# Key-block differences and the scaling of a head pair's outputs, moved between two engines of a four-layer transformer kernel

## The chip, the cores and the metric

The kernel runs on one NeuronCore of a Trainium2 chip. Its engines work side by side and meet at semaphores: TensorE (PE, with its weight loads shown apart as PEld), VectorE (DVE), ScalarE (ACT), GpSimd (POOL), and the DMA queue of SyncE (SP). The metric is the device time of one execution in microseconds (us); lower is better.

## The reference, cut to what matters

Four layers of attention and feed-forward over one sequence of 2048 positions and width 128, each with a layer norm ahead and a residual behind. Three of the attention blocks are softmax attention with 16 heads of 64: one plain, one causal, one with a region mask and a bias by feature. In short:

```python
Q = jnp.einsum('btd,hkd->bthk', x, W_Q) + b_Q
K = jnp.einsum('btd,hkd->bthk', x, W_K) + b_K
V = jnp.einsum('btd,hkd->bthk', x, W_V) + b_V
scores = jnp.einsum('bqhk,bshk->bhqs', Q, K) / jnp.sqrt(jnp.asarray(d_head, x.dtype))
# second block: dot = jnp.where(causal, dot, -inf); last block: region mask and a bias
attn = jax.nn.softmax(scores, axis=-1)
out_h = jnp.einsum('bhqs,bshk->bqhk', attn, V)
return jnp.einsum('bqhk,hdk->bqd', out_h, W_O) + b_O
```

The feed-forward blocks are a mixture of eight experts, a gated channel mix, a ternary and a binarised two-layer network. The change doesn't touch them, nor the short algebraic attention of the third layer.

## The kernel before, in words

The three softmax blocks are one program, built three times from a table of when each piece of work is due (`LAYERS`, here called attention 0, 1 (causal) and 2). Each walks through 8 pairs of heads; the two heads of a pair share the 128 partitions (64 each). The 2048 queries are cut into four chunks of 512 (c = 0 to 3), the keys into tiles of 128. A pair takes 16 cycles in attention 0 and 2, and 10 in attention 1; a cycle (number g within the pair) handles four key tiles:

- PE multiplies the scores of a tile as a sum of products (`Kh·Qh`, `Kh·Ql`, `Kl·Qh`, and a product of auxiliary rows that carries the row maxima and masks), ACT takes the exponentials into a ring of eight tiles (`work`, L1000), DVE adds them up into the sum of a chunk (`acc`, L1230 and L1242), PE multiplies them with `V`.
- The row maxima come ahead of the scores, in units: PE multiplies queries with the difference of each two neighbouring key tiles (`Kd`, matmul `ps<-Kd,Qh`), ACT keeps the positive part (L1008, into `over` or, for a cycle's second unit, into `wexp`), PE then multiplies the queries with the first tile of each two (the "base", matmul `ps<-Kh,Qh`), and DVE adds both and takes the maximum (`tops`, L1264: two instructions per segment, results in `mpart` and at a row's end in `mcol`). In the causal block POOL cuts the blocks on the diagonal (L1110 in a unit, L1123 in the exponentials).
- While a pair is worked on, the projections of the next pair are made one by one. For a chunk of K or Q: PE multiplies, ACT writes the high part (`Kh`, `Qh`, L972), DVE the rest (`Kl`, `Ql`, L1177), and for K the difference of neighbouring tiles (`Kd`, L1181).
- When a chunk of queries is through, PE sums `acc` over the partitions, ACT copies the sums, SP packs them (`dcomp`), DVE inverts them (L1206), SP spreads the inverses over all partitions (`rden`), and one cycle later the chunk's outputs `oT` are scaled into `oN` (L1212, function `normalise`). PE multiplies `oN` with the output weights, DVE adds the product to `x` (L1201).

Every engine has its own program, written in the same order of cycles. Within a cycle DVE does: the maxima of the unit in slot 0 (left from the cycle before), the last sum of the cycle before, the maxima of slot 1, a `normalise` if one is due (cycles `mul_at`: 6, 10, 14 and 2 of the next pair in attention 0 and 2; 4, 7, 0 and 2 of the next pair in attention 1), a reciprocal if due, then the sums and projection jobs mixed. The chunks of K of the next pair are due in cycles 0, 1, 2, 3 (attention 0 and 2) and 1, 3, 4, 8 (attention 1). An engine runs its instructions in order, so whatever stands ahead of the maxima on DVE delays them, and PE waits for the maxima (`top_ready`) before it may overwrite their banks. The first pair of each attention has its projections and first maxima in an `opening` with nothing else beside them.

## Time and profile before

| | |
|---|---|
| three runs | 3916.33, 3919.72, 3926.92 us (median 3919.72) |
| the profiled execution | 3920.88 us, of which its span is 3919.2 us |
| PE busy | 3633.6 us (93%) |
| DVE busy | 2901.8 us (74%) |
| ACT busy | 2270.1 us (58%) |
| POOL busy | 196.1 us (5%), 273 instructions |
| granted TensorE clock, mean | 0.972 |

The three attention blocks take 84 to 1365 us, 1508 to 2346 us and 2557 to 3858 us of the span. The layers' other work lies between. A row of a timeline is: start in us from the span's start, duration in us, engine, line, operation, output and inputs by the program's names, how many instructions, and in brackets how long the engine stood idle before it and who ended that. Two neighbouring instructions of one engine overlap a little: the next one starts before the last one's end is recorded.

### The profile page before, as it was taken

To read this page: it belongs to the slowest core of one execution; us is meant where nothing else is said; L and a number is where in the kernel's file an instruction comes from. 1 tells how busy PE (TensorE), PEld (TensorE's weight loads), DVE (VectorE), ACT (ScalarE), POOL (GpSimd) and SP (SyncE) were. 2 spreads that over 40 slices of the span, in tenths; PEclk is the share of its full clock that TensorE was granted. 3 is DMA by queue.
4 is the path that set the end of the run, shared out by engine and by line. 5 is a ranking of instruction groups with operands and counts; after the bars stand their busy time and mean duration, and the time that the engine had idled before them with its cause. 6 is when DMAs were issued, how large, how long until landed. Compare 5 with 4: busy or idle time off the path is not lost.

```text
span 3919.2 us, 65392 instructions
## 1 busy us (share of the span) xinstructions
PE 3633.6 (93%) x24661; PEld 1907.6 (49%) x24661; DVE 2901.8 (74%) x5821; ACT 2270.1 (58%) x2635; POOL 196.1 (5%) x273
## 2 busy tenths in 40 slices
PE   4999999999999958999999996699999999999997
PEld 2455455454554424555555554245545455554544
DVE  5777878778787777777777765477777877778784
ACT  3666666666666516655655652466666666666663
POOL 1000000000000001212222210000000000000000
PEclk9999999999999989999999997899999999999998
DMA  1000000000000000000000000000000000000000
GB/s 51 7 9 10 9 11 8 9 10 9 9 7 7 9 13 7 15 15 12 15 12 13 10 15 3 19 7 12 7 9 10 10 9 10 9 10 8 7 10 17
DMA packets 44398, 44.27 MB, mean 11 GB/s; under 512 B 16466, under 2 KB 30554, under 8 KB 43834
## 3 DMA queue, kind: packets, MB, share of 16 engines
q1 hardware_dynamic: 44090, 40.09, 3.3%
q8 instruction: 202, 3.31, 0.3%
q14 instruction: 106, 0.87, 0.1%
HBM read 37.56 MB, written 1.70 MB: 10 GB/s over the span
## 4 chain that ended last, share of the span: by engine, by line
PE 79%; DVE 11%; issue 4%; ACT 3%; DMA 1%; SPq 1%; POOL 0%; DVEq 0%; ACTq 0%
PE ps L565 76%; DVE over L1264 2%; DVE acc L1242 2%; DVE wexp L1264 1%; DVE x L1402 1%; ACT Kh L972 1%; ACT work L1000 1%; PE ps L863 1%; PE ps L874 1%; DVE stats L1150 1%; DVE Kd L1181 1%; PE ps L554 1%; SPq L475 0%; PE ps L903 0%; DMA auxQ<-mrow 0%
## 5 line engine op out<-in xcount | busy, mean ns | idle before, releaser
L1000 ACT ACTIVATE work<-ps 128x1024 f32<-128x1024 f32 (+1 forms) x1344 | 1276.8, 994 | 950.6 <-PE ps L565 943.9
L1242 DVE TENSOR_TENSOR acc<-acc,work 128x1024 f32<-128x1024 f32 (+2 forms) x1152 | 1353.5, 1175 | 49.4 <-ACT work L1000 11.8
L565 PE MATMUL ps<-work,V 128*64 128x512 f32 (+3 forms) x5376 | 1239.9, 581 | 0.0
L565 PEld LDWEIGHTS ps<-work,V 128*64 128x64 f32 x5376 | 452.8, 138 | 547.2 <-issue 452.7
L565 PE MATMUL ps<-Qh,Kh 64*128 64x512 f32 (+3 forms) x2688 | 654.2, 482 | 32.4 <-issue 10.8
L1264 DVE CUSTOM_DVE_ANT_0 over<-ps,over,mpart 128x512 f32<-128x512 f32 (+3 forms) x642 | 422.3, 695 | 310.4 <-PE ps L565 310.2
L565 PE MATMUL ps<-Qh,Kl 64*128 64x512 f32 (+3 forms) x2688 | 525.7, 385 | 0.0
L565 PE MATMUL ps<-Ql,Kh 64*128 64x512 f32 (+3 forms) x2688 | 522.5, 383 | 0.0
L565 PE MATMUL ps<-auxQ,auxK 64*128 64x512 bf16 (+3 forms) x2688 | 518.6, 380 | 0.0
L1264 DVE CUSTOM_DVE_ANT_0 wexp<-ps,wexp 128x512 f32<-128x512 f32 (+1 forms) x632 | 376.5, 635 | 24.1 <-PE ps L565 19.2
L565 PE MATMUL ps<-Kh,Qh 64*128 64x512 f32 (+2 forms) x1520 | 343.1, 464 | 35.8 <-DVE mpart L1264 14.5
L1008 ACT ACTIVATE over<-ps 128x1024 f32<-128x1024 f32 (+1 forms) x321 | 314.2, 979 | 26.3 <-PE ps L565 26.3
L1008 ACT ACTIVATE wexp<-ps 128x1024 f32<-128x1024 f32 x318 | 328.3, 1032 | 0.0
L565 PE MATMUL ps<-Kd,Qh 64*128 64x512 f32 (+2 forms) x1504 | 289.2, 454 | 38.9 <-DVE mpart L1264 29.5
L565 PEld LDWEIGHTS ps<-Qh,Kh 64*128 64x128 f32 x2688 | 260.1, 188 | 125.1 <-ACT work L1000 60.3
L565 PEld LDWEIGHTS ps<-Kh,Qh 64*128 64x128 f32 x1520 | 139.4, 186 | 337.3 <-issue 236.2
L565 PEld LDWEIGHTS ps<-auxQ,auxK 64*128 64x128 bf16 x2688 | 133.0, 93 | 345.3 <-issue 342.2
L565 PEld LDWEIGHTS ps<-Qh,Kl 64*128 64x128 f32 x2688 | 255.6, 185 | 51.5
L565 PEld LDWEIGHTS ps<-Ql,Kh 64*128 64x128 f32 x2688 | 258.2, 187 | 19.9
L565 PE MATMUL ps<-yT,wqk 128*64 128x512 f32 x768 | 214.0, 616 | 13.3 <-DMA wqk<-in_wqk 12.3
L565 PEld LDWEIGHTS ps<-Kd,Qh 64*128 64x128 f32 x1504 | 142.3, 188 | 131.9 <-DVE mpart L1264 62.2
L1177 DVE SCALAR_TENSOR_TENSOR Ql<-ps,bqk,Qh 128x512 fp32r<-128x512 f32 x96 | 72.0, 750 | 167.8 <-ACT Qh L972 167.8
(188 smaller groups left out, 2599.3 us busy)
## 6 DMA issues: line engine op xcount, KB each, us to landing
rden<-inverse_sums SPq DMA_DIRECT2D x192, 128.0 KB, 2.8
auxQ<-mrow SPq DMA_DIRECT2D x384, 1.0 KB
wqk<-in_wqk SPq DMA_DIRECT2D x24, 128.0 KB, 2.5
dcomp<-rden SPq DMA_DIRECT2D x192, 2.0 KB
wv<-in_wv SPq DMA_DIRECT2D x24, 64.0 KB, 2.3
inverse_sums<-rcomp SPq DMA_DIRECT2D x96, 4.0 KB, 1.3
work<-in_mlp_w SPq DMA_DIRECT2D x1, 1024.0 KB
work<-in_c_aux SPq DMA_DIRECT2D x1, 1024.0 KB, 4.9
```

The costliest lines, as they stand in the source:

```text
L554: mm = pe.transpose(ps[:, t // TPC, (t % TPC) * P:(t % TPC + 1) * P], work[:, t // TPC, (t % TPC) * P:(t % TPC + 1) * P], ident[:])
L565: return pe.matmul(o, w, m, start=start, stop=stop, skip_group_check=True)
L863: pe.matmul(bank(m % 4), wm[:, 2 * n, j * P:(j + 1) * P], yv[:, c * CH:(c + 1) * CH], start=True, stop=True).then_inc(s["h_psum"], 1)
L874: mm = pe.matmul(ps[:, 4 + c, t * P:(t + 1) * P], work[:, j * 4 + c, t * P:(t + 1) * P], wm[:, 2 * n + 1, j * P:(j + 1) * P], start=(j == ...
L972: act.activation(dst[p][:, c * CH:(c + 1) * CH], bank(b), ACT.Identity, bias=bqk[:, p, w:w + 1]).then_inc(s["hi_ready"], 1)
L1000: act.activation(work[:, 2 * e:2 * e + 2, q0:CH], ps[:, b:b + 2, q0:CH], ACT.Exp, scale=L.scale).then_inc(s["p_ready"], 1)
L1008: act.activation(excess_of(sl)[:, :, 0:w], ps[:, b:b + 2, 0:w], ACT.Relu)\
L1150: ins = dve.bn_stats(stats[:, t, :], x[:, t, :])
L1177: dve.scalar_tensor_tensor(lo[:, cols], bank(b), bqk[:, p, w:w + 1], hi[:, cols].bitcast(F32), ALU.add, ALU.subtract).then_inc(s["lo_ready ...
L1181: dve.tensor_tensor(Kd[p][:, c * (CH // 2):(c + 1) * (CH // 2)].rearrange("p (n k) -> p n k", k=P), tiles[:, 2 * c:2 * c + 2, 1 - L.base, ...
L1242: dve.tensor_tensor(o, o, work[:, slots[two]:slots[two] + 2, q0:CH], ALU.add).then_inc(s["acc_ready"], 1)
L1264: dve.tensor_tensor_reduce(clipped[:, h2, col:col + w], ps[:, b0 + h2, col:col + w], clipped[:, h2, col:col + w], 1.0, start, ALU.add, ALU ...
```

## The change

POOL now runs a program for all three attention blocks instead of the causal one alone. It computes the differences `Kd` and the scaling `oN`, both with its `tensor_tensor`; the same two instructions are gone from DVE. The waits stay with the moved instructions: `Kd` on the high part of K (`hi_ready`), `oN` on the spread inverses (`rden_in`), on the output's copy (`o_ready`) and on the product with the last `oN` (`op_ready`). In POOL's cycle the scaling stands first, then the diagonal cuts, then the cuts of the units, then the differences. (The blank and re-indented lines of the diff change nothing else.)

```diff
--- before.py
+++ after.py
@@ -1092,27 +1092,43 @@
                 pool.memset(selq[h2 * DH:h2 * DH + 1, 0:NREG], 1.0).then_inc(cleared, 1)
             pool.wait_ge(cleared, 3)
 
-            def cuts(L):
+            def attention(L):
+
 
 
                 s = A[L.n]
                 K = L.K
-                zero, low = pool.to_reg(0.0), pool.to_reg(-BIG)
                 none = selq[:, P - 1:P].rearrange("p (m o) -> p m o", m=1).to_broadcast([P, 2, P])
+
+                def differences(h, c):
+                    p = h % 2
+                    pool.wait_ge(s["hi_ready"], 8 * h + L.qk_index("K", c) + 1)
+                    tiles = Kh[p][:].bitcast(F32).rearrange("p (n two k) -> p n two k", two=2, k=P)
+                    pool.tensor_tensor(Kd[p][:, c * (CH // 2):(c + 1) * (CH // 2)].rearrange("p (n k) -> p n k", k=P),
+                                       tiles[:, 2 * c:2 * c + 2, 1 - L.base, :], tiles[:, 2 * c:2 * c + 2, L.base, :],
+                                       ALU.subtract).then_inc(s["kd_ready"], 1)
+
+                def normalise(h, c):
+                    pool.wait_ge(s["rden_in"], 32 * (NC * h + c + 1))
+                    pool.wait_ge(s["o_ready"], NC * h + c + 1)
+                    at_least(pool, s["op_ready"], NC * h + c)
+                    pool.tensor_tensor(oN[:], oT[:, c % 2, :], rden[:], ALU.mult).then_inc(s["on_ready"], 1)
 
                 def cut_unit(h, u, slot):
                     if L.cuts_to[u + 1] > L.cuts_to[u]:
                         pool.wait_ge(s["relu_ready"], L.NR * h + L.relus_to[u] + 1)
-                    for _, t, col, b, nb, _, ends in L.units[u]:
-                        if ends:
-                            o = excess_of(slot)[:, :, col + (nb - 1) * P:col + nb * P]
-                            last_alone = t % 2 == 0
-                            pool.affine_select(o, none if last_alone else o, [[0, 2], [-1, P]], ALU.is_ge,
-                                               low if last_alone else zero, base=0, channel_multiplier=1)\
-                                .then_inc(s["unit_cut"], 1)
+                        for _, t, col, b, nb, _, ends in L.units[u]:
+                            if ends:
+                                o = excess_of(slot)[:, :, col + (nb - 1) * P:col + nb * P]
+                                last_alone = t % 2 == 0
+                                pool.affine_select(o, none if last_alone else o, [[0, 2], [-1, P]], ALU.is_ge,
+                                                   low if last_alone else zero, base=0, channel_multiplier=1)\
+                                    .then_inc(s["unit_cut"], 1)
 
                 def cycle(x):
-                    if L.main(x):
+                    for m, c in L.due(L.mul_at, x):
+                        normalise(m, c)
+                    if L.main(x) and L.causal:
                         for j in range(4):
                             tile = 4 * x + j
                             _, q0, diag = L.steps[2 * (x % L.G) + j // 2][1][j % 2]
@@ -1124,14 +1140,21 @@
                                     .then_inc(s["diag_cut"], 1)
                     for sl, m, u in L.units_in(x):
                         cut_unit(m, u, sl)
-
-                for what, u, _, b in L.opening_items():
+                    for sl, kind, m, c in L.jobs_in(x):
+                        if kind == "K":
+                            differences(m, c)
+
+                for what, u, c, b in L.opening_items():
                     if what == "unit":
                         cut_unit(0, u, int(b != MAXB))
+                    elif u == "K":
+                        differences(0, c)
                 for at in range(L.X):
                     cycle(at)
 
-            cuts(LAYERS[1])
+            zero, low = pool.to_reg(0.0), pool.to_reg(-BIG)
+            for L in LAYERS:
+                attention(L)
 
 
         @block.vector
@@ -1176,11 +1199,6 @@
                         hi, lo, w = (Qh[p], Ql[p], 0) if kind == "Q" else (Kh[p], Kl[p], 1)
                         dve.scalar_tensor_tensor(lo[:, cols], bank(b), bqk[:, p, w:w + 1], hi[:, cols].bitcast(F32),
                                                  ALU.add, ALU.subtract).then_inc(s["lo_ready"], 1)
-                        if kind == "K":
-                            tiles = Kh[p][:].bitcast(F32).rearrange("p (n two k) -> p n two k", two=2, k=P)
-                            dve.tensor_tensor(Kd[p][:, c * (CH // 2):(c + 1) * (CH // 2)].rearrange("p (n k) -> p n k", k=P),
-                                              tiles[:, 2 * c:2 * c + 2, 1 - L.base, :], tiles[:, 2 * c:2 * c + 2, L.base, :],
-                                              ALU.subtract).then_inc(s["kd_ready"], 1)
                     elif kind == "mt":
                         top = ps[0:2 * TPC, b, 0:P]
                         dve.wait_ge(s["mt_psum"], NC * h + c + 1)
@@ -1204,12 +1222,6 @@
                 def inverse(h, c):
                     dve.wait_ge(s["comp_in"], 32 * (NC * h + c + 1))
                     dve.reciprocal(rcomp[:], dcomp[:]).then_inc(s["inv_ready"], 1)
-
-                def normalise(h, c):
-                    dve.wait_ge(s["rden_in"], 32 * (NC * h + c + 1))
-                    dve.wait_ge(s["o_ready"], NC * h + c + 1)
-                    at_least(dve, s["op_ready"], NC * h + c)
-                    dve.tensor_tensor(oN[:], oT[:, c % 2, :], rden[:], ALU.mult).then_inc(s["on_ready"], 1)
 
                 def sums_of(x):
 
@@ -1284,8 +1296,6 @@
                     for sl, m, u in before_:
                         if sl == 1:
                             tops(m, u, slot=1)
-                    for m, c in L.due(L.mul_at, x):
-                        normalise(m, c)
                     for m, c in L.due(L.inv_at, x):
                         inverse(m, c)
                     for which in sums[:1]:
```

The programs of PE, ACT and SP are the same row for row. DVE's has 201 rows fewer, POOL's has 116 more.

On DVE, in cycles 2 and 3 of a pair in attention 0 (`Kl` belongs to the next pair, `over` and `mcol` to the row maxima). Before:

```order
L1242 TENSOR_TENSOR acc<-acc,work 128x1024
L1177 SCALAR_TENSOR_TENSOR Kl<-ps,bqk,Kh 128x512
L1181 TENSOR_TENSOR Kd<-Kh 128x256
L1242 TENSOR_TENSOR acc<-acc,work 128x1024
L1264 ISA over,mcol<-ps,over,mpart 128x512
L1264 ISA mcol 128x1
```

And now:

```order
L1200 SCALAR_TENSOR_TENSOR Kl<-ps,bqk,Kh 128x512
L1254 TENSOR_TENSOR acc<-acc,work 128x1024
L1276 ISA over,mcol<-ps,over,mpart 128x512
L1276 ISA mcol 128x1
L1276 ISA over,mcol<-ps,over,mpart 128x512
```

The sum and the maxima follow the low part of K at once; line numbers have shifted.

On POOL, in cycles 0 to 2 of a pair in attention 1 (`work` are the diagonal cuts of the exponentials, `over` those of a unit). Before:

```order
L1123 AFFINE_SELECT work<-work 128x2x128 [waits p_ready_1] x4
L1110 AFFINE_SELECT over<-over 128x2x128 [waits relu_ready_1]
L1110 AFFINE_SELECT over<-selq 128x2x128 [waits relu_ready_1]
L1123 AFFINE_SELECT work<-work 128x2x128 [waits p_ready_1] x4
L1110 AFFINE_SELECT over<-over 128x2x128 [waits relu_ready_1]
```

And now:

```order
L1139 AFFINE_SELECT work<-work 128x2x128 [waits p_ready_1] x4
L1124 AFFINE_SELECT over<-over 128x2x128 [waits relu_ready_1]
L1124 AFFINE_SELECT over<-selq 128x2x128 [waits relu_ready_1]
L1107 TENSOR_TENSOR Kd<-Kh 128x256 [waits hi_ready_1]
L1115 TENSOR_TENSOR oN<-oT,rden 128x512 [waits op_ready_1,o_ready_1,rden_in_1]
L1139 AFFINE_SELECT work<-work 128x2x128 [waits p_ready_1] x4
L1124 AFFINE_SELECT over<-over 128x2x128 [waits relu_ready_1]
```

The difference of cycle 1 and the scaling of cycle 2 now stand between two units' cuts and the four diagonal cuts of cycle 2.

## Rows read from the trace of the kernel before

**Rows 1.** The page: the chain that ended last, share of the span by engine.
```profile
PE 79%; DVE 11%; issue 4%; ACT 3%; DMA 1%; SPq 1%; POOL 0%; DVEq 0%; ACTq 0%
```

**Rows 2.** Windows of attention 0, 1, 2: length; PE, PEld, DVE, ACT, POOL busy; clock; DMA.
```profile
84.00:1365.00 1281.00, 1264.70 (x8446) 639.15 (x8444) 1004.68 (x1729) 810.12 (x903) 0.00 (x0) 1.00 0.03 9
1508.00:2346.00 838.00, 784.22 (x6032) 450.02 (x6030) 609.65 (x1450) 495.84 (x616) 178.79 (x243) 0.98 0.04 13
2557.00:3858.00 1301.00, 1278.45 (x8746) 652.03 (x8744) 1009.09 (x1738) 811.92 (x903) 0.00 (x0) 1.00 0.03 9
```

**Rows 3.** Waits in attention 0 (us, times, longest); the last row reads alike in attention 2.
```profile
DVE Kl L1177 <- ACT Kh L972: 50.6, 28, 3.2
...
PE ps L565 <- DVE mcol L1264: 5.3, 15, 0.4
```

**Rows 4.** Waits in attention 1.
```profile
PE ps L565 <- DVE mpart L1264: 35.9, 50, 1.3
```

**Rows 5.** Timeline, attention 0, end of cycle 2 and start of cycle 3.
```profile
598.62 0.75 DVE L1177 SCALAR_TENSOR_TENSOR Kl<-ps,bqk,Kh 128x512 fp32r<-128x512 f32 x1 [1.47 <-ACT Kh L972]
599.29 0.41 DVE L1181 TENSOR_TENSOR Kd<-Kh 128x256 fp32r<-128x256 f32 x1
...
599.51 0.50 PE L565 MATMUL ps<-Kh,Qh 64*128 64x512 f32 x2
...
599.62 1.22 DVE L1242 TENSOR_TENSOR acc<-acc,work 128x1024 f32<-128x1024 f32 x1
...
600.76 0.75 DVE L1264 CUSTOM_DVE_ANT_0 over<-ps,over,mpart 128x512 f32<-128x512 f32 x1
...
602.24 0.50 PE L565 MATMUL ps<-Kh,Qh 64*128 64x512 f32 x2 [0.38 <-DVE mcol L1264]
```

**Rows 6.** Timeline, attention 1, end of cycle 1 and start of cycle 2.
```profile
1846.10 0.75 DVE L1177 SCALAR_TENSOR_TENSOR Kl<-ps,bqk,Kh 128x512 fp32r<-128x512 f32 x1 [1.41 <-ACT Kh L972]
1846.76 0.41 DVE L1181 TENSOR_TENSOR Kd<-Kh 128x256 fp32r<-128x256 f32 x1
...
1847.87 0.41 POOL L1123 TENSOR_SCALAR_AFFINE_SELECT work<-work 128x256 f32<-128x256 f32 x1 [3.94 <-ACT work L1000]
...
1848.59 1.22 DVE L1242 TENSOR_TENSOR acc<-acc,work 128x1024 f32<-128x1024 f32 x1
1848.73 0.50 PE L565 MATMUL ps<-Kh,Qh 64*128 64x512 f32 x2 [0.76 <-DVE mpart L1264]
...
1851.21 0.46 PE L565 MATMUL ps<-Kd,Qh 64*128 64x256 f32 x2 [1.14 <-DVE mpart L1264]
```

**Rows 7.** Timeline, attention 1: two cuts on POOL, asked of POOL alone.
```profile
1768.52 0.41 POOL L1110 TENSOR_SCALAR_AFFINE_SELECT wexp<-selq 128x256 f32<-128x256 bf16 x1 [1.66 <-ACT wexp L1008]
1768.88 1.39 POOL L1110 TENSOR_SCALAR_AFFINE_SELECT wexp<-wexp 128x256 f32<-128x256 f32 x1
```

**Rows 8.** Timeline, the same stretch, asked of DVE alone.
```profile
1768.57 1.43 DVE L1242 TENSOR_TENSOR acc<-acc,work 128x1024 f32<-128x1024 f32 x1
```

**Rows 9.** Timeline, attention 0, DVE and the DMA queue: cycles 1 and 2.
```profile
747.88 1.14 SPq L489 DMA_DIRECT2D rden<-inverse_sums  x2
...
749.87 2.55 DVE L1242 TENSOR_TENSOR acc<-acc,work 128x1024 f32<-128x1024 f32 x2
...
756.03 0.69 DVE L1212 TENSOR_TENSOR oN<-oT,rden 128x512 f32<-128x512 f32 x1
```

**Rows 10.** DMA issues: KB each, median us from issue to landing.
```profile
rden<-inverse_sums SPq DMA_DIRECT2D x192, 128.0 KB, 2.8
```

**Rows 11.** Timeline, opening of attention 0: the first product with the differences.
```profile
56.74 0.69 ACT L972 ACTIVATE Qh<-ps,bqk 128x512 fp32r<-128x512 f32 x1 [0.17 <-PE ps L565]
...
58.30 0.50 PE L565 MATMUL ps<-Kd,Qh 64*128 64x512 f32 x2 [1.60 <-DVE Kd L1181]
```

**Rows 12.** The chain in order of time, end of attention 0.
```profile
1376.99 0.70 DVE oN L1212
...
1377.83 1.99 PE ps L565 x16
```

## The prediction

> **What bounds the kernel now.** I read the windows of the three attention blocks first. They hold 3420 of 3919 us, and in attention 0 and 2 PE is busy 1264.70 of 1281 and 1278.45 of 1301 us, with DVE at 78% [rows 2]. There only 16 and 23 us are left to be won on PE. Attention 1 is the looser one: PE is busy 784.22 of 838 us, 54 us are left, and DVE has only 73%. So DVE is nowhere full; what counts is where PE waits for one result of it. The chain that ended last agrees: 79% PE, 11% DVE [rows 1]. Next the waits. In attention 0 PE stands 5.3 us in 15 waits behind the maxima `mcol`, the same in attention 2, and in attention 1 it stands 35.9 us in 50 waits behind the maxima `mpart` [rows 3, 4]. Last the timelines of those waits, to see what stands ahead of the maxima on DVE.
>
> In attention 0 it is this: DVE waits 1.47 us for `Kh`, makes `Kl`, then `Kd`, then one sum, and only then both maxima of `over`. PE waits 0.38 us for them at 602.24, though its base product (599.51, 0.50 long) was ready at 600.01 and the first maximum began at 600.76 [rows 5]. This happens behind the cycles 2 and 3, in which the last two chunks of K are due: 2 times for each of the 7 next pairs, 14 times, which fits the 15 waits. In attention 1 `Kd` stands directly ahead of the maxima, and PE waits 0.76 us and then 1.14 us [rows 6]; three of the four chunks of K there are due at a cycle's end, so 3 x 7 = 21 times.
>
> **The differences on DVE go.** There are 3 x 8 x 4 = 96. Each is recorded with 0.41 us, but its step in DVE's stream, start to start, is 599.62 - 599.29 = 0.33 us [rows 5], and 1847.10 after 1846.76 reads the same. Only that step can be given back.
> - Attention 0: 14 x 0.33 = 4.6 us, since the wait of 0.38 us is longer than the step. After the move the maxima would start at 600.43, still behind PE's 600.01, so the whole step arrives. A smaller wait behind cycle 1 gives perhaps 0.1 x 7 = 0.7 us. Sum 5.3 us.
> - Attention 2, whose row of waits reads the same: 5.3 us.
> - Attention 1: 21 x 0.33 = 6.9 us.
> - The other 96 - 12 - 49 = 35 differences lie where DVE waits for ACT or PE next; nothing comes back there.
>
> **The openings.** In attention 0 PE waits 1.60 us for the fourth `Kd` until 58.30 [rows 11]. DVE makes `Kl` and `Kd` in turn; GpSimd makes only `Kd`, from each `Kh` on. The first product also needs `Qh`, which ends at 56.74 + 0.69 = 57.43; with 0.15 us for the hand-over PE starts at about 57.6, 0.7 us earlier. Twice that for attention 2, and for attention 1, with one difference ahead of PE instead of four, I give 0.3 us (estimate). Sum 1.7 us.
>
> **The scalings on DVE go.** They are also 96, of 0.69 or 0.70 us [rows 9, 12]. They stand behind the maxima of their cycle, ahead of sums, and DVE comes to the next maxima with idle time; PE waits for `mpart` and `mcol`, not for sums. I cost their removal at nothing, and hold up to 2 us of gain as the good end.
>
> **What GpSimd takes for them.** The trace has no two-input instruction on GpSimd. The nearest is the diagonal cut, one input, 256 columns: 0.41 us alone [rows 7]. How much of it is reading can be seen beside it: a DVE sum that started 0.05 us after the cut took 1.43 us [rows 8] instead of 1.22 [rows 5]. So the cut held up a sum by 0.21 us and 256 columns of one input are read in about 0.21 us (0.8 ns per column), with 0.20 us fixed. From below, `Kd` costs no less than the cut, 0.41 us, and `oN` no less than on DVE, 0.69 us. From above, twice and four times the cut: 0.82 and 1.64 us. I take fixed part plus reads: `Kd` 0.20 + 2 x 0.21 = 0.62 us, `oN` 0.20 + 4 x 0.21 = 1.04 us. The first is nearest to its row. The Trainium skill (GPSIMD Engine Reference, Elementwise — side-by-side cycle accounting) has 4497 ns for 2048 columns, which as an estimate would make about 0.56 and 1.12 us of the columns alone; no run here shows it yet, and the sum below would be worse by under 1 us with it.
>
> **Whom that disturbs.** The next cut on GpSimd, 1768.88, took 1.39 us instead of 0.41 [rows 7]: it stood behind the DVE sum, which also reads two operands from SBUF. So the two block each other, in both directions, and the question is what DVE runs while GpSimd reads.
> - `Kd` on GpSimd can start when `Kh` is there, and this is when `Kl` starts on DVE: DVE waited for `Kh` in all 28 cases of attention 0 (50.6 us) [rows 3]. `Kl` reads one operand from PSUM. Its step is 0.67 us (598.62 to 599.29), so with 0.62 us `Kd` is over when the sum begins. Upper end, 0.82 us: the sum waits some 0.15 us, 28 times in attention 0 and 2, 4.2 us lost.
> - `oN` can start when `rden` lands: second issue at about 748.5, 2.8 us more, 751.3 [rows 9, 10]. DVE runs two sums from 749.87 to 752.42, in the new order from 749.54 to 752.1. GpSimd waits for the second one and runs beside the maxima (PSUM and one SBUF operand). DVE ran this scaling at 756.03, so there are 4 us of slack for the product that needs it.
> - In attention 1 GpSimd now has `Kd` and then `oN` ahead of the four cuts of cycle 2. `Kh` is there at 1846.1, so they end at 1846.1 + 0.62 + 1.04 = 1847.8; the first cut began at 1847.87 [rows 6]. Just in time. A cut that begins a little later would still be reading when the sum of 1848.59 (in the new order 1848.26) starts, and what follows that sum are maxima that PE waits for: I charge the 0.21 us of a cut's reading for most of the 7 pairs, 1.2 us.
> - At the end of each attention nothing hides the scaling: `oN` 0.70 us, then PE [rows 12]. 3 x (1.04 - 0.70) = 1.0 us lost; upper end 2.8 us.
>
> The rule that speaks against this change is in the Trainium skill (SBUF — State Buffer, Who interferes with whom): a DVE instruction with two SBUF inputs and a GpSimd instruction that reads SBUF exclude each other, the one that comes second being blocked until the first one has finished. The trace agrees for GpSimd as the second; as the first, it held the sum up by 0.21 us of its 0.41, so only while it reads. By the full length `Kd` would still be over with `Kl`, and the sum stays.
>
> **Sum.** 5.3 + 5.3 + 6.9 + 1.7 - 1.2 - 1.0 = 17.0 us gained. With the low ends of GpSimd's times it is 19 us (21 with 2 us for the scalings), with the high ends 5.3 + 5.3 + 6.9 + 1.7 - 4.2 - 1.2 - 2.8 = 11.0 us. The profiled execution took 3920.88 us, 1.2 above the median of 3919.72; the sum against it gives 3903.9, and against the median, which I predict from, 3902.7: 3903 us.
>
> **Rivals.**
> - No change that can be told (3908 to 3931; a measurement of this kernel tells 0.3%, 12 us). Something takes back what is won: GpSimd's times are at their upper ends, or `oN` slips in between two sums. With 1.04 us held, the sum behind it starts 1 us late; in cycle 1 to 2 of [rows 9] DVE has no idle time before the maxima at all, so PE would lose up to 1 us, 14 times in attention 0 and 2. 17 - 14 leaves 3 us: 3917. For it: `rden` lands within a microsecond of a gap between sums. Against: the landing lies inside the second sum, not ahead of it.
> - Slower: GpSimd's difference is far slower than its cut, say 1.4 us (for instance because it writes the rounded 32-bit format, which no GpSimd row here does). Then it still reads when `Kl` is through, and the sum starts at 598.62 + 1.4 = 600.0 instead of 599.62: the maxima are 0.4 us later than before, 28 times, 11 us, plus the lost gain; in attention 1 `Kd` and `oN` together last over 3.5 us and the cuts of cycle 2 come 2 us late, of which PE would see about 1 us 7 times; the three ends cost 5 us (2.5 us for `oN` instead of 0.7), the openings 1.5 us each; the 6.9 us of attention 1 stay won. 3919.7 + 11 + 7 + 5 + 3 - 7 = 3939. It decides from about 1.0 us of `Kd` on: 0.67 us of `Kl` plus the 0.33 us that the step gives back. Against it: the cut's 0.41 us.
> - More than I count: in attention 1, PE's waits total 35.9 us, and maxima that come earlier might also free sums and exponentials behind them. 25 us, 3895.
>
> **How the numbers follow.** Forecast (gain 11 to 20 us, 3899 to 3909) 0.52; more 0.06; no change 0.30; slower 0.12. Faster by over 0.3% means under 3908: nearly all of the forecast and the third rival, 0.57. Within 0.3%: 0.31. Slower: 0.12. The range leaves out the slower case and part of the larger gain: 3894 to 3924.
>
> **What would show it.** No `Kd` or `oN` on DVE; DVE busy down by 96 x (0.41 + 0.69) = 106 us, POOL up by 96 x (0.62 + 1.04) = 160 us. In attention 0, DVE's sum starts right behind `Kl`, about 0.67 us after it, and PE's 5.3 us for `mcol` nearly vanish. In attention 1 PE's wait for `mpart` falls by 6 us. The window of attention 0 shortens by 6 us, of attention 1 by 6, of attention 2 by 5. Wrong it would be if DVE's sums grow above 1.22 us on the average, if `Kd` on GpSimd takes over 1 us, or if PE's waits name POOL.

## The result, and the profile after

The changed kernel takes 3900.66 us (median of 10 runs, 3897.33 to 3907.19) against 3919.17 us before (10 runs, 3911.76 to 3926.92). The medians are 18.5 us apart, 0.47%. The measured ratio is 0.9945, with a 95% interval of 0.9928 to 0.9963. The forecast was 3903 us. The two profiled executions have spans of 3919.2 and 3899.2 us, 20.0 us apart, and all comparisons of stretches below add up to that.

The page first: busy time and the chain that ended last, to be read against [rows 1].

```profile
PE 3622.7 (93%) x24661; PEld 1905.0 (49%) x24661; DVE 2820.0 (72%) x5629; ACT 2270.6 (58%) x2635; POOL 393.5 (10%) x465
...
PE 81%; DVE 10%; issue 4%; ACT 3%; DMA 1%; SPq 1%; POOL 0%; POOLq 0%; DVEq 0%; ACTq 0%
```

DVE is busy 82 us less (forecast 106) and POOL 197 us more (forecast 160); PE has 2 points more of the chain and DVE one less. PE does the same 24661 matmuls in 3622.7 us of busy time instead of 3633.6. So 10.9 of the 20.0 us are matmuls that ran faster, and 9.1 us are PE standing less. The windows of the three attentions after (columns as in [rows 2]):

```profile
84.00:1362.00 1278.00, 1266.14 (x8454) 638.87 (x8452) 982.15 (x1671) 809.87 (x903) 67.13 (x59) 1.00 0.03 9
1502.00:2333.00 831.00, 778.80 (x6112) 448.07 (x6112) 589.14 (x1411) 502.72 (x623) 231.23 (x306) 1.00 0.05 13
2544.00:3838.00 1294.00, 1274.78 (x8722) 649.50 (x8720) 984.30 (x1676) 809.05 (x900) 67.90 (x59) 1.00 0.03 9
```

In attention 1 the granted clock reads 1.00 instead of 0.98. That small difference turns out to be the largest single part of the result. The edges of such windows are chosen by hand, so for the lengths I take the first and the last start of the exponentials (line L1000) in each attention. In the kernel before:

```profile
L1000 ACT ACTIVATE work<-ps x512: 1020/1025/1031, 84.1 to 1364.0; 128x1024 f32<-128x1024 f32 x171
...
L1000 ACT ACTIVATE work<-ps x320: 378/1024/1029, 1508.3 to 2345.4; 128x1024 f32<-128x1024 f32 x128, 128x512 f32<-128x512 f32 x32
...
L1000 ACT ACTIVATE work<-ps x512: 1019/1025/1032, 2557.3 to 3857.0; 128x1024 f32<-128x1024 f32 x171
```

And after:

```profile
L1000 ACT ACTIVATE work<-ps x512: 1019/1025/1032, 83.7 to 1358.8; 128x1024 f32<-128x1024 f32 x171
...
L1000 ACT ACTIVATE work<-ps x320: 378/1024/1031, 1507.3 to 2324.2; 128x1024 f32<-128x1024 f32 x128, 128x512 f32<-128x512 f32 x32
...
L1000 ACT ACTIVATE work<-ps x512: 1020/1025/1033, 2540.2 to 3836.5; 128x1024 f32<-128x1024 f32 x171
```

| stretch | before | after | gained | forecast |
|---|---|---|---|---|
| ahead of attention 0 | 84.1 | 83.7 | 0.4 | openings, 1.7 in all |
| attention 0 | 1279.9 | 1275.1 | 4.8 | 5.3 |
| between 0 and 1 | 144.3 | 148.5 | -4.2 | -0.3 (one end) |
| attention 1 | 837.1 | 816.9 | 20.2 | 6.9 - 1.2 |
| between 1 and 2 | 211.9 | 216.0 | -4.1 | -0.3 |
| attention 2 | 1299.7 | 1296.3 | 3.4 | 5.3 |
| behind attention 2 | 62.2 | 62.7 | -0.5 | -0.3 |

The total was right, its parts only half: attention 1 gave three times what was forecast, and the stretches between the attentions took 8.3 us back.

PE's waits, first in attention 0 (against [rows 3]), then in attention 1 (against [rows 4]):

```profile
PE ps L565 <- DVE mcol L1276: 0.2, 1, 0.2
```

```profile
PE ps L565 <- DVE mpart L1276: 31.8, 51, 1.4
```

In attention 0 the 5.3 us are gone; in attention 1 only 4.1 of 35.9 us are, so 20.2 us cannot be waiting time. PE between the first and the last exponential of attention 1, before and after (columns as in [rows 2]), shows where they are:

```profile
1508.34:2345.38 837.04, 783.26 (x6026) 449.46 (x6024) 608.69 (x1448) 495.33 (x614) 178.17 (x243) 0.98 0.04 13
```

```profile
1507.32:2324.23 816.91, 767.13 (x6026) 441.91 (x6024) 581.60 (x1390) 495.44 (x615) 227.00 (x301) 1.00 0.04 13
```

The same 6026 matmuls are busy 16.1 us less, and PE stands 4.0 us less (53.8 and 49.8 us). The timeline of attention 1 at the place of [rows 6] (pair 3, cycles 1 and 2, first DVE, then POOL, then PE):

```profile
1837.41 0.75 DVE L1200 SCALAR_TENSOR_TENSOR Kl<-ps,bqk,Kh 128x512 fp32r<-128x512 f32 x1 [1.40 <-ACT Kh L972]
1838.08 0.61 DVE L1276 CUSTOM_DVE_ANT_0 over<-ps,over,mpart 128x384 f32<-128x384 f32 x1
...
1839.58 1.30 DVE L1254 TENSOR_TENSOR acc<-acc,work 128x1024 f32<-128x1024 f32 x1
```

```profile
1837.46 0.73 POOL L1107 TENSOR_TENSOR Kd<-Kh 128x256 fp32r<-128x256 f32 x1 [2.23 <-ACT Kh L972]
1838.15 1.28 POOL L1115 TENSOR_TENSOR oN<-oT,rden 128x512 f32<-128x512 f32 x1
1839.39 0.41 POOL L1139 TENSOR_SCALAR_AFFINE_SELECT work<-work 128x256 f32<-128x256 f32 x1
```

```profile
1839.71 0.50 PE L565 MATMUL ps<-Kh,Qh 64*128 64x512 f32 x2 [0.44 <-DVE mpart L1276]
...
1842.27 0.84 PE L565 MATMUL ps<-Kd,Qh 64*128 64x256 f32 x6 [1.21 <-DVE mpart L1276]
1843.04 1.08 PE L565 MATMUL ps<-acc,ones 128*64 128x512 f32 x4
```

`Kl` is followed by the maxima at once, and PE's first wait falls from 0.76 to 0.44 us: the step of 0.33 us, as forecast. The second one rises from 1.14 to 1.21, because `oN` on POOL ends at 1839.43, the first cut follows 0.2 us late (1.98 us behind the start of `Kl`, before 1.77) and lengthens the sum of 1839.58 to 1.30 us. So the waits of this cycle gain 0.25 us. But the cycle, from its first exponential to the next cycle's, went from 14.4 to 12.6 us. Where the rest lies, four matmuls later, is shown by the same work in the kernel before:

```profile
1851.21 1.13 PE L565 MATMUL ps<-Kd,Qh 64*128 64x256 f32 x6 [1.14 <-DVE mpart L1264]
1852.27 1.97 PE L565 MATMUL ps<-acc,ones 128*64 128x512 f32 x4
```

The four matmuls of `acc` took 1.97 us there and take 1.08 now. The windows show the granted clock of that stretch, before:

```profile
1846.80:1851.20 4.40, 2.31 (x26) 1.75 (x26) 4.40 (x16) 2.69 (x4) 2.37 (x4) 1.00 0.00 0
1851.40:1854.80 3.40, 3.40 (x12) 1.20 (x12) 2.70 (x3) 1.53 (x3) 0.41 (x1) 0.50 0.02 5
```

and after:

```profile
1838.10:1842.20 4.10, 2.31 (x26) 1.73 (x26) 4.10 (x15) 2.71 (x4) 3.40 (x6) 1.00 0.00 1
1842.20:1845.60 3.40, 3.33 (x18) 1.43 (x20) 2.11 (x4) 2.46 (x3) 0.81 (x1) 1.00 0.02 5
```

Before, PE had been busy 2.31 of 4.40 us and then ran at 1.2 GHz; after, it had been busy 2.31 of 4.10 us and stayed at 2.4 GHz. The trace of before has 12 such stretches in attention 1, in cycles 2 and 9 of a head pair (41.0 us in all), that of after has 2 (6.8 us). One of the two, with the same place of the cycle ahead of it, is this:

```profile
1731.50:1735.60 4.10, 2.30 (x26) 1.73 (x26) 4.10 (x15) 2.65 (x4) 3.35 (x6) 1.00 0.00 1
1735.60:1739.00 3.40, 3.39 (x12) 1.47 (x14) 2.05 (x2) 1.25 (x2) 0.53 (x1) 0.51 0.00 0
```

PE did there what it did in the cycle above, 2.30 of 4.10 us, and yet the clock fell. So these figures alone don't tell when it falls; they tell what a fall costs. The four matmuls take 1.98 us there; the cycle lasts 14.1 us, the cycles 2 at full clock 12.6 us. A stretch costs 1.5 us and ten of them 15 us, which fits the 16.1 us of busy time; the remaining 4 us of the 20.2 are the waits.

### The profile page after: what moved, and what is told of

It is laid out like the page before. It is cut to its first block, busy times and chain, and to the rows that moved or that the text cites. A ratio compares the mean times of both kernels' runs of the same rounds, so it can differ in the third digit from the quotient of the medians.

```text
span 3899.2 us, 65392 instructions
## 1 busy us (share of the span) xinstructions
PE 3622.7 (93%) x24661; PEld 1905.0 (49%) x24661; DVE 2820.0 (72%) x5629; ACT 2270.6 (58%) x2635; POOL 393.5 (10%) x465
## 4 chain that ended last, share of the span: by engine, by line
PE 81%; DVE 10%; issue 4%; ACT 3%; DMA 1%; SPq 1%; POOL 0%; POOLq 0%; DVEq 0%; ACTq 0%
PE ps L565 77%; DVE over L1276 2%; DVE wexp L1276 2%; DVE acc L1254 1%; DVE x L1412 1%; ACT work L1000 1%; PE ps L863 1%; PE ps L874 1%; ACT Kh L972 1%; PE ps L554 1%; DVE stats L1173 1%; SPq L475 0%; PE ps L903 0%; ACT Qh L972 0%; DMA auxQ<-mrow 0%
## 5 line engine op out<-in xcount | busy, mean ns | idle before, releaser
L1000 ACT ACTIVATE work<-ps 128x1024 f32<-128x1024 f32 (+1 forms) x1344 | 1276.7, 995 | 930.8 <-PE ps L565 923.3
L1115 POOL TENSOR_TENSOR oN<-oT,rden 128x512 f32<-128x512 f32 x96 | 140.6, 1464 | 1842.2 <-DMA rden<-inverse_sums 1842.2
```

The costliest lines, as they stand in the source:

```text
L1000: act.activation(work[:, 2 * e:2 * e + 2, q0:CH], ps[:, b:b + 2, q0:CH], ACT.Exp, scale=L.scale).then_inc(s["p_ready"], 1)
L1115: pool.tensor_tensor(oN[:], oT[:, c % 2, :], rden[:], ALU.mult).then_inc(s["on_ready"], 1)
```

## The experiments

Times are medians; each ratio is against the kernel before, run on the same chip. The kernel before took 3918.4 us beside the halves apart, the later difference and the step put back; 3919.9 beside the long difference, the ends on VectorE and the moved sum; and 3921.4 beside the scaling by attention and the last kernel, so differences of up to 3 us between kernels of different groups tell nothing.

**The two halves apart.** With the differences alone on GpSimd, the scaling is in its old place on VectorE:

```diff
 # GpSimd, cycle(x)
-                    for m, c in L.due(L.mul_at, x):
-                        normalise(m, c)
 # VectorE, ahead of the reciprocals
+                    for m, c in L.due(L.mul_at, x):
+                        normalise(m, c)
```

> Only the differences are on GpSimd; the scaling is back on VectorE. Theory (the whole gain comes from the step that the differences leave on VectorE, and most of it from PE's clock in attention 1, which no longer falls after the shortened waits): all of the gain stays and the three ends are 0.6 us shorter each, so 3897 to 3901 us; attention 1 lasts about 817 us with at most 3 windows of half clock. Rival (VectorE gains by having fewer instructions altogether, the scaling's 66 us included): only 40 of 106 us of relief are left, so the time lies nearer to the kernel before, about 3912 us.

Measured: 3888.89 us (3887.26 to 3892.18), ratio 0.9928 [0.9911, 0.9944]. This is 11.8 us less than the changed kernel and 8 us under the range of my theory. By the exponentials the attentions take 1274.2, 814.4 and 1294.4 us: 5.7, 22.7 and 5.3 us less than before. So the differences are worth 30 us and not 18, and the scaling's move, which I had costed at nothing beside 1.0 us at the ends, takes 12 back.

The other half, the scaling on GpSimd and the differences on VectorE behind `Kl`:

```diff
 # VectorE, job(kind, ...)
                         dve.scalar_tensor_tensor(lo[:, cols], ...)
+                        if kind == "K":
+                            dve.tensor_tensor(Kd[p][...], tiles[...], tiles[...], ALU.subtract)
```

> Only the scaling is on GpSimd; the differences are back on VectorE. Theory: no gain, 3919 us plus 2 us for the three ends and a few microseconds for VectorE sums that wait behind a scaling (16 such sums in attention 0 and 2 of the changed kernel, 6.5 us in all): 3919 to 3926 us, and 12 or more windows of half clock in attention 1. Rival (fewer instructions on VectorE): 66 of 106 us of relief, about 3908 us.

Measured: 3939.13 us (3934.22 to 3944.61), ratio 1.0054 [1.0038, 1.007]. Slower than before by 21 us, well outside what I expected. PE's waits in attention 1 grew from 35.9 us to

```profile
PE ps L565 <- DVE mpart L1276: 45.8, 52, 1.5
```

I had expected 12 or more stretches at the lower clock in attention 1. There are 6, two of them of double length, 27.3 us in all against 41.0 before. More waiting did not mean more time at the lower clock here.

**Place or engine?** Nothing but the cuts on GpSimd; VectorE makes `Kd` not behind `Kl` but behind the next cycle's maxima.

```diff
-                        if kind == "K":
-                            dve.tensor_tensor(Kd...)
+                        if kind == "K":
+                            late.append((h, c))     # in the openings: at once
...
+                    while late:                     # behind both maxima of the next cycle
+                        difference(*late.pop(0))
```

> GpSimd does what it did before. The differences stay on VectorE, but outside the openings each is made in the next cycle, behind that cycle's maxima, instead of ahead of them. Theory (what counts is the place ahead of the maxima, not the engine): the steady part of the gain stays, only the openings lose their 1.5 us, and the ends are the short ones: 3898 to 3903 us, half clock in attention 1 in at most 3 windows. Rival (the engine must be relieved): VectorE is as busy as before, 3919 us.

Measured: 3893.39 us (3891.35 to 3897.07), ratio 0.9938 [0.9923, 0.9952], 5 us under the range of my theory, with 4 stretches at the lower clock in attention 1 where I had expected at most 3. VectorE does as much as before and the kernel is 25 us faster, faster than the changed one. What is won is the place ahead of the maxima; GpSimd adds 4.5 us to that at most.

**The step put back.** The changed kernel, and VectorE makes the difference once more at the old place, into a spare tile that nobody reads, in attention 1 alone.

```diff
+                        if kind == "K" and L.causal:
+                            dve.tensor_tensor(spare..., tiles[...], tiles[...], ALU.subtract)
```

> The changed kernel, and in attention 1 alone VectorE also makes the differences once more, at their old place, into a tile that nobody reads. Theory (a step of 0.33 us ahead of the maxima makes PE's waits long enough that its clock falls behind them): attention 1 goes back to about 837 us with 10 or more windows of half clock, in all 3916 to 3922 us; attention 0 and 2 stay at 1276 and 1297 us. Rival (the extra 14 us of attention 1 have nothing to do with the step, for instance a lucky phase of the clock): only 28 x 0.33 = 9 us are lost at most, 3905 to 3910 us, and few windows of half clock.

Measured: 3915.75 us (3911.21 to 3923.36), ratio 0.9993 [0.9982, 1.0004]: 15 us of the gain are gone with 32 instructions (4 of them in the opening) of a 0.33 us step. The time lies just under the 3916 to 3922 us of my theory. Attention 1 is 17 us longer than after, with 8 stretches at the lower clock instead of 2 (I had expected 10 or more), and its window reads 0.98 again:

```profile
1503.00:2338.00 835.00, 777.68 (x6032) 447.47 (x6030) 593.57 (x1420) 496.23 (x616) 235.64 (x301) 0.98 0.05 13
```

21 of these steps stand ahead of maxima, 6.9 us. The other 10 us are what the clock makes of them: between its first and last exponential PE is busy 9.8 us more than after, for the same matmuls, and stands 7.5 us more.

**Does a long instruction of GpSimd hold a sum?** The difference made twice in one instruction (512 columns; the second copy goes to spare columns of `Kd`).

```diff
+                    twice = Kd[p][:].rearrange("p (r n k) -> p r n k", n=2, k=P)[:, c:NC + 1:NC - c, :, :]
+                    pool.tensor_tensor(twice, both[0], both[1], ALU.subtract)
```

> The changed kernel (3900.7 us), with the difference on GpSimd made twice in one instruction (the second copy goes to spare columns), so some 1.4 us long instead of 0.73 us. Theory of the slower rival in the prediction (a GpSimd instruction with two SBUF inputs blocks a sum with two SBUF inputs until it has finished; break-even at about 1.0 us): the sum behind Kl starts 1.4 us after Kl instead of 0.67 us, 42 times in attention 0 and 2; the maxima behind it are 0.4 us later than in the kernel before, so PE waits 0.7 to 0.8 us for mcol in 28 of them; attentions 0 and 2 each 10 to 13 us longer than in the changed kernel, attention 1 some 3 us longer for later cuts: 3921 to 3930 us. Rival (the sum starts when it likes and is only slowed while the two run together): the sum starts 0.67 us after Kl and lasts 1.3 to 1.9 us instead of 1.22 us, PE loses 0.1 to 0.7 us in each place: 3903 to 3918 us. Second rival (GpSimd alone pays, its instruction gets longer): no change, 3900 to 3902 us.

Measured: 3929.44 us (3925.45 to 3936.56), ratio 1.0025 [1.0016, 1.0034]: 29 us more than after. DVE, POOL and PE in attention 0:

```profile
288.56 0.75 DVE L1202 SCALAR_TENSOR_TENSOR Kl<-ps,bqk,Kh 128x512 fp32r<-128x512 f32 x1 [1.34 <-ACT Kh L972]
289.23 1.73 DVE L1256 TENSOR_TENSOR acc<-acc,work 128x1024 f32<-128x1024 f32 x1
290.88 0.74 DVE L1278 CUSTOM_DVE_ANT_0 over<-ps,over,mpart 128x512 f32<-128x512 f32 x1
```

```profile
288.61 1.28 POOL L1111 TENSOR_TENSOR Kd<-Kh 128x512 fp32r<-128x512 f32 x1 [9.32 <-ACT Kh L972]
```

```profile
292.36 0.50 PE L565 MATMUL ps<-Kh,Qh 64*128 64x512 f32 x2 [0.49 <-DVE mcol L1278]
```

The sum is recorded from 289.23, as in the changed kernel, but lasts 1.73 us instead of 1.21: 0.52 us longer, while `Kd` still ran for 0.66 us of it. This is the price of the rival that ended slower, by its mechanism; the sum's record shows the delay as length and not as a late start, so the first of my expectations had the form wrong and the size nearly right. Attention 0 and 2 are 10 us longer than after each, and the opening 4.6 us. With the real 0.73 us, `Kd` ends when `Kl` does (0.67 us) and none of the sums behind `Kl` in the changed kernel is longer than 1.22 us.

**Where does the scaling cost?** First the scalings behind the last main cycle of each attention back to VectorE, the rest on GpSimd:

```diff
 # GpSimd
+                    for m, c in L.due(L.mul_at, x) if L.main(x) else []:
 # VectorE
+                    for m, c in [] if L.main(x) else L.due(L.mul_at, x):
```

> The changed kernel (3900.7 us), with the scalings that fall behind the last main cycle of each attention back on VectorE; those in the steady part stay on GpSimd. The kernel with all scalings on VectorE and the differences on GpSimd took 3888.9 us, so the scaling's move costs 11.8 us; in its trace the two stretches between attentions are 2.6 and 4.3 us shorter and the tail 1.1 us, the three attentions 0.9, 2.5 and 1.8 us. Theory (the cost sits at the ends: nothing hides 1.26 us there instead of 0.69 us, and TensorE stands longer, so that it comes back at the lower clock): 8 us come back, 3892 to 3894 us, and TensorE's waits for the scaling on GpSimd (22.1 us in 3 waits) are gone. Rival (the cost sits in the steady part, by sums of VectorE that the scaling holds up to 1.1 us): at most 3 x 0.6 = 2 us come back, 3898 to 3900 us.

Measured: 3898.79 us (3897.2 to 3905.29), ratio 0.9951 [0.9939, 0.9964]. The ends are worth 1.9 us, of 11.8. That is less than these times can tell from nothing, but PE's three waits at the ends agree with it: 22.1 us in the changed kernel, 20.2 us here. The rival holds for the time: the cost lies elsewhere. Then by attention, with attention 1's scalings on VectorE and the rest on GpSimd, and the reverse:

```diff
-                    for m, c in L.due(L.mul_at, x):                    # GpSimd
+                    for m, c in L.due(L.mul_at, x) if not L.causal else []:   # reverse: if L.causal
```

> The changed kernel (3900.7 us) with the scalings of attention 1 alone back on VectorE. All scalings on VectorE gave 3888.9 us, the last ones of each attention on VectorE only 3898.8 us, so most of the 11.8 us lies in the steady part. Theory (sums of VectorE held up by the scaling, and each place where PE then waits longer; they were 10, 13 and 6 in the attentions 0, 1 and 2, of 3.4, 2.8 and 3.2 us): every attention has its share, attention 1 some 2.5 us of it and the stretch ahead of it 2.6 us: 3895 to 3898 us. Rival (the cost sits in attention 1 alone, where the scaling stands ahead of the four cuts and of maxima that PE waits for): all of it comes back, 3888 to 3891 us.

> The opposite: the scalings of attention 1 alone on GpSimd, those of attention 0 and 2 on VectorE. Theory (every attention has its share): 3892 to 3896 us, and with the kernel before this one the two costs add up to some 12 us. Rival (attention 1 alone): 3898 to 3901 us. A third outcome, both under 3893 us, would say that the cost is no sum of its parts and hangs on where PE's clock falls in the stretches between the attentions (58 and 101 us at the lower clock with the scaling on GpSimd, 51 and 95 us without).

Measured: 3894.37 us (3890.52 to 3899.08), ratio 0.9933 [0.9918, 0.9947], and 3897.5 us (3894.32 to 3899.21), ratio 0.994 [0.9926, 0.9953]. Over the 3888.9 us without any scaling on GpSimd, attentions 0 and 2 cost 5.5 us and attention 1 costs 8.6 us; together 14, against 11.8 for all. Taken each against the kernel before of its own group, they cost 2.5 and 5.6 us, together 8, against 11.0. So the cost is spread, with the larger part in attention 1; how large each part is these runs leave open by some 3 us. How it comes about can be seen in attention 0 of the changed kernel, DVE, POOL and PE:

```profile
994.68 1.95 DVE L1254 TENSOR_TENSOR acc<-acc,work 128x1024 f32<-128x1024 f32 x1
```

```profile
994.26 1.29 POOL L1115 TENSOR_TENSOR oN<-oT,rden 128x512 f32<-128x512 f32 x1 [40.84 <-DMA rden<-inverse_sums]
```

```profile
997.90 0.74 PE L565 MATMUL ps<-Kd,Qh 64*128 64x512 f32 x4 [0.53 <-DVE mpart L1276]
```

The scaling began beside the maxima of `over` and still ran for 0.87 us when the sum began; the sum took 0.73 us more than its 1.22, the next maxima came late, and PE waited. In the three attentions 10, 13 and 6 sums are lengthened, by 3.4, 2.8 and 3.2 us in all (before, 7 in attention 1 by 1.5 us). Of the 13 in attention 1, 8 run beside a cut and only 5 beside a scaling. Shortest, median and longest sum of attention 0 and 1 in ns:

```profile
L1254 DVE TENSOR_TENSOR acc<-acc,work x448: 1148/1220/2112, 88.2 to 1360.6; 128x1024 f32<-128x1024 f32 x150
...
L1254 DVE TENSOR_TENSOR acc<-acc,work x256: 416/1215/2339, 1512.8 to 2327.1; 128x1024 f32<-128x1024 f32 x96, 128x512 f32<-128x512 f32 x32
```

This explains a part of the 12 us. Against the trace with the differences alone, the three attentions are 0.9, 2.5 and 1.8 us longer, 5.2 in all, and PE stands idle as much longer in them. Another 7.0 us lie in the two stretches between the attentions, 5.6 of them in PE's busy time, for the same number of matmuls. The mean granted clock of all executions is nearly the same, 0.9744 (ten of the changed kernel) and 0.9748 (five with the differences alone), so I can't say that the clock takes these 7 us as a rule; where they come from is not shown.

**What else stands ahead of the maxima?** In the trace with the differences alone on GpSimd, PE still waits 1.14 us in cycle 2 and 1.30 us in cycle 9 of attention 1, each time behind maxima that follow a sum. The last sum of the cycle before was moved behind them, once with the differences on GpSimd and once with all on VectorE:

```diff
-                    for which in last:
+                    for which in last if not L.causal else []:
                         add(*which)
...                                  # behind the maxima of slot 1
+                    for which in last if L.causal else []:
+                        add(*which)
```

> The kernel with the differences on GpSimd and the scaling on VectorE (3888.9 us), and in attention 1 the last sum of the cycle before moved behind the maxima of slot 1 instead of ahead of them. In its trace that sum (a step of 1.14 us) stands directly ahead of the maxima of wexp in the cycles 2 and 9 of a head pair, and PE waits 1.14 and 1.30 us behind these, 14 times in all. Theory (only what stands ahead of the maxima costs, whatever it is): the waits nearly vanish, 14 x 1.14 = 16 us, and the two low stretches of the clock that are left in attention 1 go: 3870 to 3874 us. Rival (the cuts on GpSimd or the exponentials' ring are late next, because the sums come 1.5 us later): under 6 us, 3883 to 3889 us.

> The same move of the last sum in attention 1, on top of the kernel in which nothing is on GpSimd but the cuts and VectorE makes the difference behind the next cycle's maxima (3893.4 us). Theory: as with the differences on GpSimd, 16 us less, 3875 to 3879 us; VectorE has about 25% idle time in attention 1, so it stays 2 to 6 us behind the kernel with the differences on GpSimd, by the openings and the longer queue of sums. Rival (VectorE, with difference, sum and scaling now all behind the maxima, is late for the exponentials' ring): 3884 to 3893 us.

Measured: 3885.42 us (3878.53 to 3889.01), ratio 0.9912 [0.9898, 0.9925], and 3889.74 us (3888.42 to 3892.12), ratio 0.9926 [0.9913, 0.994]. 3.5 and 3.7 us instead of 16: my theory was too simple. What took the sum's place, DVE and PE of the first one, in cycle 2:

```profile
1731.41 0.75 DVE L1280 CUSTOM_DVE_ANT_0 wexp<-ps,wexp,mpart 128x512 f32<-128x512 f32 x1 [0.71 <-PE ps L565]
```

```profile
1730.76 0.50 PE L565 MATMUL ps<-Kh,Qh 64*128 64x512 f32 x2 [0.43 <-DVE mpart L1280]
...
1732.90 0.84 PE L565 MATMUL ps<-Kd,Qh 64*128 64x256 f32 x6 [0.81 <-DVE mpart L1280]
```

DVE now stands idle 0.71 us for the product that starts at 1730.76, on which these maxima work. The sum had filled that time; only what it exceeded it by, 1.14 - 0.81 = 0.33 us, could be won. The move also made cycle 5 longer, by 0.6 to 0.9 us. Without it there:

```diff
-                    for which in last if L.causal else []:
+                    for which in last if L.causal and x % L.G != 5 else []:
```

> The kernel with the differences on GpSimd, the scaling on VectorE and the last sum of attention 1 moved behind the maxima of slot 1 (3885.4 us), but not in cycle 5 of a head pair, where that move made the cycle 0.77 us longer (10.50 to 11.27 us) and only cycle 6 0.52 us shorter. Theory: 7 x 0.25 = 1.8 us less, 3883 to 3884 us. Rival: the order within attention 1 does not matter any more, 3885 to 3886 us; if the move in cycle 5 is what feeds cycle 7 (0.27 us shorter), 3887 us.

Measured: 3877.31 us (3873.21 to 3879.55), ratio 0.9886 [0.9869, 0.9902]: the fastest of all, 23 us under the changed kernel and 8 us under the one with the move everywhere, over four times what I expected. Its trace has 1 stretch at the lower clock in attention 1 where the one before had 5. PE stands 40.2 us in attention 1 where it stood 40.3, and is busy 764.8 us where it was 772.6: nearly all of the gain is the clock. The five stretches and the one come at the same place of cycle 9, and PE's last waits ahead of each are the same, 0.43 and 0.94 us, as in the pairs in which the clock does not fall. So which pairs it falls in is not decided by these waits alone, and a part of the 8 us may be luck.

## Why the prediction was right, and where its parts were not

**Attention 0 and 2, 5.3 us each.** Right, step by step: with the differences moved alone they gain 5.7 and 5.3 us, and PE's waits for `mcol` vanish. In the changed kernel it is 4.8 and 3.4 us, because the scaling takes some back.

**Attention 1, 6.9 minus 1.2 us.** The mechanism was right (21 steps of 0.33 us; cuts that come just in time and touch a sum), the size was not: 20.2 us. The term lacks PE's clock. The step put back in attention 1 took 17 us there, of which 6.9 are the steps. In the traces of the three kernels with the step ahead of the maxima PE has 27.3 to 41.0 us at the lower clock in attention 1, and their mean granted clocks over all executions are 0.971 to 0.9725; in those of the ten kernels without it it has 3.4 to 17.1 us, and the means are 0.9735 to 0.9766. The Trainium skill (TensorE: Matmul & The Clock Gate, Part 1: The HAM clock gate) says that TensorE's rate is set by how busy it has been of late; the traces agree in the main, with 12 stretches at 0.50 before and 2 after, but not in each case, as the kernel with the scaling alone shows. [rows 2] had shown 0.98 for attention 1 beside 1.00 for the others. I took that figure as given; 0.02 of 838 us is 17 us at full rate, and that was the hint of what might be won or lost with the waits. The third rival (25 us) had the right place for more gain, but another cause. The cut that touches a sum, charged at 1.2 us, made PE's wait in cycle 2 longer by 0.08 us in six pairs, 0.5 us in all.

**The openings, 1.7 us.** 0.4 us in attention 0. The first product with `Kd` starts at 57.86 instead of 58.30 [rows 11], with `Qh` late next, as forecast; I had hoped for 57.6.

```profile
57.86 0.50 PE L565 MATMUL ps<-Kd,Qh 64*128 64x512 f32 x2 [0.83 <-ACT Qh L972]
```

**The scalings go from DVE, "at nothing".** This is the step that failed. The move cost 12 us on this base and 21 us on that of the kernel before; of it I had only the 1.0 us of the ends. Nothing on DVE or PE waits for the scaling's result in the steady part, as I had said (PE's waits name POOL `oN` at the ends alone, 22.1 us in 3 waits where `oN` on DVE had been named for 19.7). But I had argued, from one cycle and from the median landing of `rden`, that GpSimd would wait for a sum and then run beside the maxima. It does start beside maxima, and where it starts late in them it is still reading when the next sum begins. That was my "no change" rival, and it came true in part: 29 sums are lengthened, 21 of them beside a scaling and 8 beside a cut. So the differences gave 30 us where their terms (5.3 + 5.3 + 6.9 + 1.7 - 1.2) made 18, and the scaling took 12 where its term made 1. The two misses, 12 and 11 us, cancelled. That the total came out within 3 us is luck.

**GpSimd's times.** `Kd` 0.73 us, forecast 0.62 within 0.41 to 0.82; `oN` alone 1.26 to 1.29 us, forecast 1.04 within 0.69 to 1.64. The means of all, with what blocking adds:

```profile
L1115 POOL TENSOR_TENSOR oN<-oT,rden 128x512 f32<-128x512 f32 x96 | 140.6, 1464 | 1842.2 <-DMA rden<-inverse_sums 1842.2
...
L1107 POOL TENSOR_TENSOR Kd<-Kh 128x256 fp32r<-128x256 f32 x96 | 70.1, 730 | 1107.1 <-ACT Kh L972 1106.7
```

`Kd` is never lengthened (0.72 to 0.74 us in all 96): in the attentions it nearly always falls beside `Kl`. The break-even of 1.0 us for it is not contradicted: 0.73 us costs nothing, 1.28 us costs 29 us, and nothing between was run. The way to these forecasts had an error. I had taken the 0.21 us by which a cut held up a sum as its reading time. That cut and the sum overlapped by 0.35 us; in the changed kernel, at 1839.58, they overlap by 0.22 us and the sum is 0.08 us longer. Both are the overlap less 0.14 us, as behind `Kd` and `oN`. So the hold says where the two met and not how long the cut reads.

**The ends, 1.0 us.** 1.9 us by the experiment. The chain at the end of attention 0 against [rows 12]:

```profile
1372.22 1.27 POOL oN L1115
1373.49 0.14 issue
1373.63 1.99 PE ps L565 x16
```

**Between the attentions, 8.3 us lost.** Not in the prediction at all, beside the ends. In these stretches PE is often at the lower clock. The two of before, and below them those of after:

```profile
1365.00:1508.60 143.60, 93.67 (x414) 46.27 (x410) 102.92 (x365) 34.61 (x57) 4.38 (x11) 0.82 0.04 11
2346.00:2557.50 211.50, 137.12 (x631) 73.98 (x629) 108.72 (x335) 76.64 (x104) 1.83 (x3) 0.78 0.04 13
```

```profile
1360.00:1507.00 147.00, 95.59 (x410) 49.20 (x406) 100.35 (x358) 34.28 (x56) 8.54 (x16) 0.80 0.04 11
2325.00:2540.00 215.00, 139.79 (x629) 76.38 (x627) 106.09 (x328) 76.64 (x103) 6.87 (x8) 0.76 0.04 12
```

The clock averages 0.02 less in both, for the same number of matmuls. By the edges of the table, 6.0 of the 8.3 us are PE's busy time and 2.3 us its idle time. The later `x` at the ends is part of it (0.6 us each). The rest does not follow the scaling from kernel to kernel: the second stretch is 211.5 us in the kernel with the ends on VectorE, and 215.4 us in that with all but the cuts on VectorE and the sum moved. I read these 4 us as two ways in which the clock can fall there, with one profiled execution of each kernel to go by. That was only argued, and it stays open how often each comes. For the same reason the 12 us of the scaling are taken from medians and not from a sum of stretches.

## What to carry to other kernels

Ask of each instruction on a helper engine what stands directly behind it for the engine that bounds: 96 differences with a step of 0.33 us, 49 of them ahead of maxima that PE waits for, were worth 30 us, and 96 scalings of 0.7 us in slack places cost nothing that could be seen on VectorE but 12 us on GpSimd. Move such a step behind the critical one on its own engine first, before giving it to an engine whose reads of SBUF hold up the first one's. Where the page shows a granted clock even slightly under 1.00 in the stage that is to be improved, work out separately what the stage would be at full clock: in attention 1, 4 us less of waiting came with 16 us less of time for the same matmuls. But count on the clock's share only as a chance, since the same waits did not always bring it down.

## What the runs showed of the hardware

- A subtraction of two SBUF operands on GpSimd, 128x256, took 0.73 us, twice the columns 1.28 us; a product of 128x512 took 1.26 to 1.29 us alone and up to 2.35 us in the way of VectorE's sums.
- Of a GpSimd instruction with two SBUF operands that is first, the VectorE sum with two SBUF operands that follows is delayed by all but the last 0.14 us (0.66 us of overlap gave 0.52 us, 0.87 gave 0.73). The cut, which has one operand, does the same: 0.35 us of overlap gave 0.21 us, 0.22 gave 0.08. The sum's record begins at once and is only longer, so the delay is seen in its duration and not in idle time. The Trainium skill (SBUF — State Buffer, Who interferes with whom) calls the shared ports "an exclusive lock", the second instruction blocked until the first has finished; these numbers bear that out but for the 0.14 us.
- The cycles 2 and 9 of attention 1 have 14 waits of PE of 1.13 to 1.30 us, before and after. Before, a stretch at 1.2 GHz began within 0.6 us of the end of 12 of them, after of only 2, though the waits themselves were as long (those of cycle 2 mostly 0.08 us longer); what had become shorter was the wait 2.5 us ahead, 0.44 us instead of 0.76. Each such stretch cost 1.5 us. It is no rule: with the step put back all 14 pairs of waits are as before, and 8 of them bring the stretch; in the kernel with the sum moved, waits of 0.43 and 0.94 us bring it 5 times. Why it comes in some pairs and not in others is open.
